# A two-layer graph product: seven block products for three of five row groups, with the extra block sums on VectorE

## What is computed

```python
h = jnp.maximum(_layernorm(x), 0.0)
u = par_u[0] * par_u[1] * (diag_u[:, None] * h[:2048] @ W_u) + h[:2048]
i = par_i[0] * par_i[1] * (diag_i[:, None] * h[2048:] @ W_i) + h[2048:]
e = jnp.concatenate([u, i], axis=0)
g = adj @ (adj.T @ e)
out = x + layernorm(g) * ln_gamma + ln_beta + h
```

## Time and profile before

| | |
|---|---|
| runs, median (lowest to highest) | 371.75 us (371.45 to 372.2) |
| profiled execution: its own time | 371.32 us |
| its span, first to last instruction | 369.5 us |
| mean granted TensorE clock | 0.997 |
| PE busy | 360.3 us (98%) |
| DVE (VectorE) busy | 263.0 us (71%) |
| POOL (GpSimd) busy | 159.6 us (43%) |
| ACT (ScalarE) busy | 74.3 us (20%) |
| loads of 1 MiB: row blocks, columns, last | 100, 20, 4 |

### The profile page before, as it was taken

How to read it: one execution, slowest core, us unless ns; L and a number is a source line. 1 busy time by engine, 2 the same in 40 slices (tenths; PEclk the granted TensorE clock), 3 DMA queues, 4 the chain that set the end, 5 groups by cost and what they waited for, 6 DMA issues and landing times.

```text
span 369.5 us, 10865 instructions
## 1 busy us (share of the span) xinstructions
PE 360.3 (98%) x4776; PEld 151.7 (41%) x4776; DVE 263.0 (71%) x282; ACT 74.3 (20%) x213; POOL 159.6 (43%) x94
## 2 busy tenths in 40 slices
PE   7998999999999999999999999999999999999994
PEld 4664454543323443443334334334433343344432
DVE  5999994999061969395677839694956768385266
ACT  5863022010050004001300500040023005002422
POOL 2023060020019902970793199049607931990036
PEclk9999999999999999999999999999999999999998
DMA  8999999999999978989898989889898989853933
GB/s 311 422 419 415 418 426 419 419 419 402 403 380 411 363 291 331 427 343 411 323 429 331 419 326 425 338 318 421 349 409 326 427 339 413 325 247 132 426 130 142
DMA packets 19897, 133.22 MB, mean 361 GB/s; under 512 B 2209, under 2 KB 2977, under 8 KB 4001
## 3 DMA queue, kind: packets, MB, share of 16 engines
q1 hardware_dynamic: 19440, 132.22, 88.1%
q10 hardware_dynamic: 432, 0.66, 0.5%
HBM read 131.55 MB, written 1.31 MB: 360 GB/s over the span
## 4 chain that ended last, share of the span: by engine, by line
PE 87%; DMA 7%; POOL 2%; SPq 2%; DVE 1%; issue 0%; ACT 0%; DVEq 0%; POOLq 0%
PE h_acc L887 36%; PE t_acc L918 24%; DMA natural<-adj_rows 7%; PE x_acc L955 7%; PE h_acc L975 7%; PE t_acc L856 5%; PE t_acc L955 5%; PE h_acc L870 2%; POOL xs L424 1%; SPq L289 1%; POOL sums L420 1%; PE t_acc L993 1%; DVE xs L795 0%; SPq L286 0%; DVE sums L784 0%
## 5 line engine op out<-in xcount | busy, mean ns | idle before, releaser
L599 DVE STREAM_TRANSPOSE strips<-natural 128x2048 f32<-128x2048 f32 x76 | 169.0, 2279 | 48.2 <-PE h_acc L887 48.0
L887 PE MATMUL h_acc<-strips,tokens 32*64 32x512 f32 x2432 | 133.5, 589 | 0.1
L918 PE MATMUL t_acc<-natural,e 128*32 128x512 f32 x832 | 92.3, 592 | 0.1
L887 PEld LDWEIGHTS h_acc<-strips,tokens 32*64 32x64 f32 x2432 | 53.3, 132 | 79.4 <-issue 74.3
L399 POOL TENSOR_TENSOR sums<-natural 128x1024 f32<-128x1024 f32 x14 | 33.3, 2381 | 113.4 <-DMA natural<-adj_rows 113.4
L918 PEld LDWEIGHTS t_acc<-natural,e 128*32 128x32 f32 x832 | 27.4, 110 | 59.4 <-issue 58.2
L955 PE MATMUL x_acc<-sums,forms 128*32 128x256 f32 x280 | 41.1, 380 | 0.0
L856 PE MATMUL t_acc<-natural,e 128*64 128x256 f32 x320 | 36.5, 382 | 1.4 <-DMA natural<-adj_rows 1.1
L489 ACT COPY smalls<-x_acc 32x256 f32<-32x256 f32 x7 | 2.6, 365 | 170.1 <-PE t_acc L955 170.1
L479 ACT COPY tokens<-tokens 32x384 f32<-32x384 f32 (+2 forms) x60 | 24.2, 403 | 51.6 <-DVE tokens L623 30.9
L407 POOL TENSOR_TENSOR sums<-natural,sums 128x1024 f32<-128x1024 f32 x14 | 33.3, 2379 | 1.1
(11 more groups left out here) (97 smaller groups left out, 299.8 us busy)
## 6 DMA issues: line engine op xcount, KB each, us to landing
natural<-adj_rows SPq DMA_DIRECT2D x100, 1024.0 KB, 7.9
cols<-adj_cols SPq DMA_DIRECT2D x20, 1024.0 KB, 11.6
natural<-adj_last SPq DMA_DIRECT2D x4, 1024.0 KB, 10.8
out<-xs SPq DMA_DIRECT2D x4, 256.0 KB, 2.0
xs<-x ACTq DMA_DIRECT2D x2, 256.0 KB, 5.3
xs<-x SPq DMA_DIRECT2D x2, 256.0 KB, 7.7
out<-xs SPq DMA_DIRECT2D x2, 128.0 KB, 2.0
smalls<-small SPq DMA_DIRECT2D x1, 150.0 KB, 3.6
```

What stands on the lines that cost most here:

```text
L599: nc.vector.transpose(strips[:, a, :, m].rearrange("p c t i -> p t c i"), natural[:, a, m].rearrange("p t (c j) -> p t c j", j=Q)).then_in ...
L887: last = nc.tensor.matmul(h_acc[D * s:D * (s + 1), q], t[part, a, b, u, :], rows, start=(isinstance(g, int) and g == 0 and b == 0 and u == 0),
L918: last = nc.tensor.matmul(t_acc[lane, pair_bank(half)].rearrange("p (a w) -> p a w", a=2), e[:, GT * m + 2 * k + s, Q * v:Q * (v + 1)], na ...
```

## The change

A third row group is summed. The summed groups are now 1, 2 and 4, the plain ones 0 and 3, and group 1 belongs to the early part of a pair: plain 0, summed 1, then (one turn of the loop later) summed 2, summed 4, plain 3. GpSimd adds the blocks of 1 and 4. VectorE adds those of 2, in the four buffers that GpSimd uses for 1: VectorE waits for the product of group 1 of the same pair, GpSimd for the product of group 2 of the pair before. The turns go through both panels in a mixed order, seven before `keep_t_pair` and one behind it. The loads of a pair begin with (0, 1), (0, 0), (1, 1). `u` and `v` move from one PSUM bank to another, and `v` is computed ahead of the first turn of t.

```diff
-ORDER = (0, 1, 4, 2, 3)
+ORDER = (0, 1, 2, 4, 3)
-TURNS = (0, 1, 3, 2)
-BEHIND = 2
-SUMMED = (4, 3)
+TURNS = ((0, 1), (0, 2), (0, 0), (1, 1), (0, 3), (1, 0), (1, 2), (1, 3))
+BEHIND = 1
+SUMMED = (1, 2, 4)
+BY_POOL = (1, 4)
+BY_DVE = 2
...
-        u, sixth_rest, _, v = (x_acc[Q * lane:Q * (lane + 1), WIDE:2 * WIDE] for lane in range(QUADRANTS))
+        sixth_rest = x_acc[Q:2 * Q, WIDE:2 * WIDE]
+        u, v = (t_acc[0:Q, 1, WIDE * n:WIDE * (n + 1)] for n in range(2))
...
-                for a in range(2):
-                    for m in range(EARLY):
-                        refill(g + a, m)
-                for m in (4, 3, 2):
-                    for a in range(2):
-                        refill(g + a, m)
+                for a, m in ((0, 1), (0, 0), (1, 1), (0, 2), (1, 0), (0, 4), (1, 4), (1, 2), (0, 3)):
+                    refill(g + a, m)
                 for a in range(2):
                     refill_cols(g - 2 + a)
+                refill(g + 1, 3)
...
-                for m in SUMMED:
+                for m, before in zip(BY_POOL, (BY_DVE, TURNED)):
                     for a in range(2):
                         pool.wait_ge(s_natural[a][m], 16 * (half + 1))
-                    pool.wait_ge(s_first, firsts_pair(half - 1, m))
+                    pool.wait_ge(s_first, firsts_pair(half - 1, before))
...
+            def add_blocks(half):
+
+                m = BY_DVE
+                for a in range(2):
+                    dve.wait_ge(s_natural[a][m], 16 * (half + 1))
+                dve.wait_ge(s_first, firsts_pair(half, EARLY - 1))
+                nc.vector.tensor_tensor(sum_of(m, 0), block_of(1, m, 0), block_of(1, m, 1),
+                                        ALU.add).then_inc(s_sums_dve, 1)
+                nc.vector.tensor_tensor(sum_of(m, 2), block_of(0, m, 0), block_of(1, m, 0),
+                                        ALU.subtract).then_inc(s_sums_dve, 1)
+                dve.wait_ge(s_sums_dve, sums_done(half, m, 1))
+                nc.vector.tensor_tensor(sum_of(m, 1), sum_of(m, 0), block_of(0, m, 0),
+                                        ALU.subtract).then_inc(s_sums_dve, 1)
+                dve.wait_ge(s_sums_dve, sums_done(half, m, 3))
+                nc.vector.tensor_tensor(sum_of(m, 3), block_of(0, m, 1), sum_of(m, 1),
+                                        ALU.subtract).then_inc(s_sums_dve, 1)
...
             with dve.Fori(FIRST_HALF + 1, LAST_HALF) as half:
                 turn_pair(half, keep_t_pair)
+                add_blocks(half + 1)
...
             def first_rest(half):
+                first_summed(half, 2)
                 first_summed(half, 4)
-                first_plain(half, 2)
-                first_summed(half, 3)
+                first_plain(half, 3)
 
             def first_early(half):
-                for m in range(EARLY):
-                    first_plain(half, m)
+                first_plain(half, 0)
+                if not isinstance(half, int):
+                    pe.wait_ge(s_v, 2 * (half - FIRST_HALF - 1))
+                first_summed(half, 1)
```

More of the change, by code:

```diff
@@ L34 @@
 LAST_HALF = LAST // 2
-ORDER = (0, 1, 4, 2, 3)
+ORDER = (0, 1, 2, 4, 3)
 EARLY = 2
-TURNS = (0, 1, 3, 2)
-BEHIND = 2
-SUMMED = (4, 3)
+TURNS = ((0, 1), (0, 2), (0, 0), (1, 1), (0, 3), (1, 0), (1, 2), (1, 3))
[3 more added lines that the diff above has]
+BY_DVE = 2
 FORMS = 4
-SUMS = 4 * len(SUMMED)
+SUMS = FORMS * len(BY_POOL)
 LEFT = 5
@@ L48 @@
 WARM = 4
-SCRATCH = 2048
+SCRATCH = 1024
 LN_EPS = 1e-5
@@ L149, in gnn_layer @@
         s_sums = sem("s_sums")
+        s_sums_dve = sem("s_sums_dve")
         s_sixth = sem("s_sixth")
@@ L192, in sums_done, with turns_of, turned_all @@
         def sums_done(half, m, n=4):
-            return SUMS * (half - FIRST_HALF - 1) + 4 * SUMMED.index(m) + n
+            if m == BY_DVE:
+                return FORMS * (half - FIRST_HALF - 1) + n
+            return SUMS * (half - FIRST_HALF - 1) + FORMS * BY_POOL.index(m) + n
         def turned_count(g, m):
-            return TURNED * g + (TURNS.index(m) if g >= PAIRED else m) + 1
+            if g < PAIRED:
+                return TURNED * g + m + 1
+            return TURNED * (g - g % 2) + turns_of(g - g % 2).index((g % 2, m)) + 1
+        def turns_of(g):
+            return [(a, m) for a, m in TURNS if g + a < LAST]
+        def turned_all(g, a):
+            if isinstance(g, int) and g < PAIRED:
+                return TURNED * (g + 1)
+            turns = turns_of(g) if isinstance(g, int) and g == LAST - 1 else TURNS
+            return TURNED * (g - a) + 1 + max(n for n, turn in enumerate(turns) if turn[0] == a)
         def block_of(a, m, s):
@@ L382, in _ @@
             pool.wait_ge(s_e_centred, GROUPS)
-            parts = e[:, GT * 3:GT * 5].rearrange("p (m k s) (v d) -> p m k s v d", m=2, s=2, v=2)
+            parts = e.rearrange("p (m k s) (v d) -> p m k s v d", m=GROUPS, s=2, v=2)
             for m in SUMMED:
-                low, high = (parts[:, m - 3, :, s] for s in range(2))
+                low, high = (parts[:, m, :, s] for s in range(2))
                 nc.gpsimd.tensor_tensor(form_of(m, 0), low[:, :, 1], low[:, :, 0], ALU.subtract).then_inc(s_forms, 1)
@@ L662, in keep_t_pair @@
                 nc.vector.tensor_tensor(uv, seventh, uv, ALU.add).then_inc(s_v, 1)
+                dve.wait_ge(s_v, 2 * (half - FIRST_HALF) - 1)
+                nc.vector.tensor_tensor(v, first_v, uv, ALU.add).then_inc(s_v, 1)
                 dve.wait_ge(s_t_left, left + 3)
                 turn_t(2 * half, 0, slice(0, WIDE))
-                dve.wait_ge(s_v, 2 * (half - FIRST_HALF) - 1)
-                nc.vector.tensor_tensor(v, first_v, uv, ALU.add).then_inc(s_v, 1)
                 dve.wait_ge(s_v, 2 * (half - FIRST_HALF))
@@ L678, in turn_pair @@
             def turn_pair(half, t_ready):
-                turn_first(half)
-                for m in TURNS[:-BEHIND]:
-                    turn_strips(2 * half + 1, 1, half, m)
+                for a, m in TURNS[:-BEHIND]:
+                    turn_strips(2 * half + a, a, half, m)
                 t_ready(half)
[L684 to L689, removed]
+                for a, m in TURNS[-BEHIND:]:
+                    turn_strips(2 * half + a, a, half, m)
+            def add_blocks(half):
[13 more added lines that the diff above has]
+                                        ALU.subtract).then_inc(s_sums_dve, 1)
             def keep_t_plain(half):
@@ L754, in _ @@
             turn_pair(FIRST_HALF, keep_t_plain)
+            add_blocks(FIRST_HALF + 1)
             with dve.Fori(FIRST_HALF + 1, LAST_HALF) as half:
                 turn_pair(half, keep_t_pair)
-            turn_first(LAST_HALF)
+                add_blocks(half + 1)
+            for a, m in turns_of(LAST - 1):
+                turn_strips(LAST - 1, a, LAST_HALF, m)
             keep_t_pair(LAST_HALF)
@@ L877, in second_strips @@
             def second_strips(g, a, blocks=range(BLOCKS)):
-                pe.wait_ge(s_strips, TURNED * (g + 1))
+                pe.wait_ge(s_strips, turned_all(g, a))
                 pe.wait_ge(s_t, g + 1)
@@ L949, in first_summed @@
                 ready(half, m)
-                pe.wait_ge(s_sums, sums_done(half, m))
+                pe.wait_ge(s_sums_dve if m == BY_DVE else s_sums, sums_done(half, m))
                 for i in range(len(LANES[0])):
@@ L1072, in _ @@
             second_loaded(PAIRED - 1, 1, PAIRED // 2 - 1)
+            pe.wait_ge(s_forms, FORMS * len(SUMMED))
             first_early(FIRST_HALF + 1)
-            pe.wait_ge(s_forms, 4 * len(SUMMED))
             with pe.Fori(FIRST_HALF, LAST_HALF - 1) as half:
```

## The result

The changed kernel takes 410.16 us (median of 4 runs, 408.44 to 411.31), the kernel before 371.98 us on the same chip: a ratio of 1.1025, interval 1.098 to 1.1069. The forecast was 404.4 us, in a range of 378 to 410. The sign was right, and so was the meeting of the two engines' additions; which wait ends a loop turn was not. The median is 5.8 us above the forecast and 0.16 us above the range, which is less than the runs differ among themselves.

What follows compares the result with a forecast made beforehand. TensorE's own work was taken to bound the kernel before; after the change, held-up additions and GpSimd's early sums. 371.32 + 3.3 (head) + 29.4 (six loop turns) + 0.4 (tail) = 404.4 us, range 378 to 410.

Steps and rivals of the forecast that it cites:

- Products: TensorE's loop: seven plain products become summed, 0.41 us less each, 2.9 in all, a turn of 33.4.
- VectorE's additions: Loop: VectorE's four additions and GpSimd's group 4 sums exclude each other, ending at 11.2; a turn takes 38.7, 4.9 more.
- The early sums: Loop: group 1's sums wait for (1, 1)'s turn and load; a turn takes at least 34.8, 1.0 above today's.
- at nothing or little: Remaining waits and loads: other loads land in time for the loop; `v` ahead of t costs 0.4 us in the tail.
- the forecast's sign of being right: Loop: TensorE idle once a turn ahead of group 1's summed product, waiting for GpSimd, about 5.3 us.
- Rival (d): TensorE's clock falls to 1.2 GHz in each gap, the product behind costs 3.02 more: 422 us; chance 0.05.
- Head: Before the loop: later loads and GpSimd's group 1 sums start the strips at 115.7 instead of 112.37, 3.3 us more.
- (a): Loop: VectorE gets the port at once or shares it; only load and GpSimd's sums bind: 381 us; chance 0.27.
- (b): Loop: VectorE holds the port through three additions, loses it before the fourth; turn 36.3, 390 us; chance 0.16.
- (c): Not slower: loads land within 3.9 us of issue; 371.7 us, down to 368.8; chance 0.06, half of it faster.
- a few gaps: Top of the range, 410 us: a few of TensorE's idle gaps cost clock.

Runs made afterwards that it cites:

- TensorE kept busy: The changed kernel with nine more matmuls per loop turn, whose product nobody reads, ahead of the early pair's first product: 408.76 us, ratio 1.0985.
- the filled kernel: The changed kernel with nine unread matmuls of 256 columns added per loop turn, where TensorE waited some 4 us: 408.76 us.
- the kernels without the exclusion: The changed kernel with VectorE's four additions replaced by one-input turns, 381.67 us; or with GpSimd's group 4 sums waiting for VectorE's additions, 384.03 us.
- the kernel with exchanged panels: Against the changed kernel: GpSimd's group 4 sums wait for VectorE, early turns and loads, panels swapped in the seven products, loaded columns moved in the tail: 375.78 us.
- the kernel with another order: The changed kernel with turns of (0,0), (1,1) and (1,0) ahead of (0,2) and (0,3), loads following that order: 400.44 us, ratio 1.0801.

## Why the prediction was right and wrong

**Products.** Right: with every wait gone a loop turn is 33.42 us, the 33.4 of the forecast.

**VectorE's additions.** The exclusion was right, read from one addition of 1.61 us near the end, and so was the alternation, which was put behind an "if"; the undisturbed 1.22 was measured as 1.23. Their end was put at 11.2 after the strips, with GpSimd's group 4 begun 2.9 ahead of them. In the first loop turn it began 2.96 ahead and the end came at 10.8; in the others GpSimd was up to 4.5 ahead, and the end came down to 9.2. With TensorE kept busy it was 11.5 to 12.0.

**The early sums.** The chain through (1, 1) was sized well where it does bind. In the turn shown of the kernel with TensorE kept busy the load takes 5.54 (forecast 5.6), the sums 9.6, and the loop turn is 39.1 on average (38.7); even there TensorE's wait for the sums is only 0.2 to 0.6 us, in five of six turns.

**The step that failed** is the sentence in "at nothing or little" by which the load of (1, 0) "lands at 26.8, where plain 0 begins at 27.0". It was worked out behind undisturbed turns of blocks, though the term above it had just put these turns 3.6 us late, and (1, 0) is loaded two places behind (1, 1). With the forecast's own numbers (1, 1) lands at 25.7 and (1, 0) at 25.7 + 2 x 2.46 = 30.6. In the turn shown it is issued 23.1 after the strips and lands at 30.6, the same by chance: the turns of blocks begin 1.5 us earlier than forecast, and the load takes 1.4 longer than the rate of 2.46 accounts for. That alone would not have moved the forecast: a plain 0 of 3.43 would be done at about 34, ahead of GpSimd's sums at 17.8 + 2.3 + 5.6 + 0.2 + 9.59 = 35.5. But TensorE waits for this load, and plain 0 behind it runs at 1.2 GHz: it is done at 37.3 in the turn shown, behind the sums at 34.0. So the load of (1, 0) and the slow plain 0, not the sums, end the turn, and the forecast's sign of being right, some 5.3 us of waiting for GpSimd ahead of the summed product, is nowhere in the loop. That turn is 26.85 up to the end of the columns, 4.0 of waiting, 6.38 of plain 0 and 3.13 of the summed product, 40.4; the six are 39.5 on average, for the forecast's 38.7.

That 38.7 comes so close is in part luck. In the changed kernel the additions end up to 2 us before the 11.2, and GpSimd's early sums are done 34.3 us after the strips on average, so the chain that was forecast would have given 34.3 + 0.2 + 3.02 = 37.5; the wait that was left out makes up the rest and more.

Rival (d) had the price of the clock, 3.02 where plain 0 lost 1.4 to 3.0, but put it on the summed product, and its sum was wrong too: it added the clock to the waiting, while in the filled kernel most of what the clock gave back went into other waits.

**Head.** Right: (1, 0) landed at 107.82 (107.7 forecast), GpSimd's sums ran from 103.09 to 112.67 (102.9 to 112.5), the strips began at 115.97 (115.7).

**Rivals.** (a), no exclusion, is out by the rows of the additions, but its 381 is what the kernels without the exclusion took (381.67, 384.03). (b), VectorE keeping its place for three additions, is out by the alternation. (c), loads landing within 3.9, is out: the shortest took 4.7.

The range allowed at its top for "a few gaps" of clock, and the clock fell behind all six gaps of the loop. That is not the whole of what is missing: with the clock kept up the kernel still takes 408.76 us.

**Open.** Some loads land later than both 4.8 us behind their issue and 2.46 behind the load ahead of them: (1, 0) in the turn shown by 1.4 us, and in one turn of the kernel with exchanged panels (1, 1) by 2.0, which cost that turn its 0.57. Why they do was not tried.

## What to carry to other kernels

Before work is given to an idle engine, ask whether it can run beside the engines that are busy then: VectorE had 5.84 us free in each turn, and four additions of 1.23 did not fit into it beside GpSimd's. When one term of a sum makes an engine late, go once more through every step that was put at nothing and stands behind that engine. And take the price of a fallen clock from an experiment with the engine kept busy, since time given back to a loop can be taken by the wait that stands next.

## What the runs showed of the hardware

- VectorE's two-input additions of 128x1024 and GpSimd's exclude each other for a whole instruction and then alternate: 1.23 becomes 3.38, 2.37 becomes 3.2 to 3.34. With one SBUF input VectorE keeps its 1.20 (a turn) or 0.67 (an addition of 64x512 with its other input in PSUM), and GpSimd its 2.37.
- TensorE's granted clock was 0.50 behind the gap of 4 us in the loop turn shown, and it stayed at 1.00 where matmuls that nobody reads filled most of such a gap. The length of the gap alone did not decide it: the clock was 0.63 on average in a product of 4.65 us behind a wait of 2.15 us (the kernel with another order), and 1.00 in plain 0 behind a wait of 3.02 us (the changed kernel's head).
